# First attention: where the fp16 halves of the probabilities are made, and in what form they are turned

## The reference, cut to what matters

```
scores = einsum('bhsr,bhlr->bhsl', q_r, k_r)
attn = softmax(scores, axis=-1)
ctx_c = einsum('bhsl,bld->bhsd', attn, kv_rope)
ctx_lat = einsum('bhsd,hkd->bshk', ctx_c, w_kc_kv)
out = ctx_lat.reshape(b, s, H * K) @ Wo.T
```

## Time and profile before

| | |
|---|---|
| time, median of 3 runs | 1847.28 us (1844.83 to 1847.87) |
| the profiled execution: its time and its span | 1844.54 us, 1842.9 us |
| first attention in the span | about 130 to 680 us |
| busy in the whole span: TensorE, VectorE, ScalarE, GpSimd | 1606.8, 1192.0, 1036.1, 611.1 us |
| mean granted TensorE clock | 0.931 |
| L1051, all normalisations | 64, 137.3 us |

### The profile page before, as it was taken

One profiled execution on the slowest core, in us unless ns is written; L12 is line 12 of the kernel. 1 busy time (PEld: TensorE's weight loads), 2 busy tenths in 40 slices (PEclk: granted clock), 3 DMA queues, 4 the chain that ended last, 5 costly groups with the idle time before them and its releaser, 6 DMA issues. The chain is left out here.

```text
span 1842.9 us, 35610 instructions
## 1 busy us (share of the span) xinstructions
PE 1606.8 (87%) x11911; PEld 998.5 (54%) x11911; DVE 1192.0 (65%) x2678; ACT 1036.1 (56%) x2563; POOL 611.1 (33%) x481
## 2 busy tenths in 40 slices
PE   4788999999999979989997777784599999999993
PEld 3655656656656545555554454553466666666661
DVE  4866797787787779688796777757633333333332
ACT  3447746746747627566574777743655555455451
POOL 4614304304304300000000222212167777777662
PEclk9789999999999989999998998776599999999996
DMA  8820120220120249787786001104356656556536
GB/s 271 285 84 9 55 75 9 62 68 10 65 65 10 69 157 333 239 280 241 227 260 227 12 2 37 36 29 114 78 108 140 150 136 140 137 129 136 131 74 225
DMA packets 143332, 226.57 MB, mean 123 GB/s; under 512 B 37857, under 2 KB 93409, under 8 KB 143032
## 3 DMA queue, kind: packets, MB, share of 16 engines
q1 hardware_dynamic: 107160, 195.90, 33.6%
q0 software_dynamic: 29344, 21.29, 7.1%
q10 hardware_dynamic: 6656, 7.11, 1.1%
HBM read 175.00 MB, written 98.80 MB: 149 GB/s over the span
## 5 line engine op out<-in xcount | busy, mean ns | idle before, releaser
L2751 PE MATMUL g_ps<-ring,xT 128*128 x1572 | 300.8, 327 | 1.1 <-issue 1.1
L1051 POOL TENSOR_TENSOR pr<-pr,sm 128x1444 f32<-128x1444 f32 (+1 forms) x64 | 137.3, 2145 | 385.9 <-DVE sm L1087 385.9
L2700 POOL DMA_INDIRECT acc<-rows,slot_sources x131 | 207.8, 1586 | 107.2 <-issue 78.7
L2857 DVE SCALAR_TENSOR_TENSOR hf<-sg,g_ps 128x192 f32<-128x192 f32 x131 | 46.4, 354 | 238.5 <-ACT sg L2806 206.3
L2751 PEld LDWEIGHTS g_ps<-ring,xT 128*128 128x128 f16 x1572 | 142.8, 98 | 71.9 <-issue 5.5
L2690 POOL DMA_INDIRECT xg<-xtab,slot_sources x131 | 138.0, 1054 | 81.3 <-issue 79.5
L2773 PE MATMUL d_ps<-ring,hT 128*128 x655 | 162.8, 379 | 1.6 <-ACT hT L2819 1.1
L1081 DVE TENSOR_REDUCE sm<-s_banks 128x2 f32<-128x722 f32 (+2 forms) x128 | 97.5, 762 | 67.3 <-PE s_banks L819 64.8
L973 ACT ACTIVATE pr<-s_banks,sm 128x361 f32<-128x361 f32 (+1 forms) x208 | 115.3, 563 | 30.7 <-DVE sm L1081 29.2
L876 PE MATMUL o_bank<-cT,N_hi 128*128 128x400 f16 x512 | 129.7, 335 | 0.0
L819 PE MATMUL s_banks<-kvp,qp 128*128 128x361 f16 (+1 forms) x624 | 116.9, 318 | 10.8 <-ACT pr L973 6.1
(11 more groups left out here) (322 smaller groups left out, 3848.1 us busy)
## 6 DMA issues: line engine op xcount, KB each, us to landing
split_f<-in_gu SPq DMA_DIRECT2D x64, 384.0 KB, 4.5
split_gu<-split_o SPq DMA_DIRECT2D x64, 384.0 KB, 3.1
ring<-split_gu SPq DMA_DIRECT2D x32, 768.0 KB
head<-in_head SPq DMA_DIRECT2D x16, 864.0 KB
tern_w<-in_tern SPq DMA_DIRECT2D x48, 256.0 KB
split_f<-in_down SPq DMA_DIRECT2D x32, 384.0 KB, 4.2
split_d<-split_o SPq DMA_DIRECT2D x32, 384.0 KB, 3.8
ring<-split_d SPq DMA_DIRECT2D x32, 256.0 KB
```

What stands on the lines that cost most here:

```text
L1051: nc.gpsimd.tensor_tensor(pr[:, s % 3, 0:n], pr[:, s % 3, 0:n], small[:, s % 3, 2, 0:n].unsqueeze(2).to_broadcast([P, n, KEYS]), ALU.mult) ...
L2700: nc.gpsimd.indirect_dma_start(out=core.acc[i % NACC][:, :], out_offset=bass.IndirectOffsetOnAxis(ap=core.sources[:, i:i + 1], axis=0), in ...
L2751: last = nc.tensor.matmul(g_ps[i % 2][:, 0:2 * INTER], xT[:, i % 2, a * KT + k, :], ring(i, (2 * k + w) * 2 * INTER, 2 * INTER), start=((k ...
```

## The change

The split is made ahead of the transposition, on rows rather than on turned columns. After normalising, which is now two instructions a step (the first two tiles, then the rest), ScalarE copies each part to fp16 and GpSimd subtracts this copy from the fp32 probabilities into a second fp16 tile (new probs_hi and probs_lo, one instruction a part each). TensorE turns both fp16 halves of each tile, into the two halves of one bank that is read as fp16, so there are twice as many transpositions. VectorE then takes a bank's both halves in one copy (probs_out). The three slots of pr become two (probs0, probs1), with two for the fp16 parts (probs_parts). They lie over single ternary tiles in an order of their own, and some waits for the ternary tiles are set accordingly. An fp16 identity is written over the bf16 one for the duration of the stage and put back after it.

```diff
+ROW_PAD = 368
+TERN_ORDER = (("w", 0), ("w", 1), ("a", 0), ("s", 0), ("m", 0), ("a", 2), ("g", 2), ("s", 2), ("w", 2), ("g", 0), ("a", 1),
+              ("g", 1), ("m", 1), ("s", 1), ("m", 2), ("o", 1), ("o", 2), ("o", 0))
...
-        pad = tern.bytes // (3 * 4 * 4)
-        assert pad >= KEYS and STEPS % 3 == 1
-        pr = core.sb(ctx, "pr", [P, 3, 4, pad], F32)[:, :, :, 0:KEYS]
+        assert STEPS % 2 == 0
+        pr = [core.sb(ctx, f"probs{p}", [P, widest, KEYS], F32) for p, widest in enumerate((4, 3))]
+        ph = [core.sb(ctx, f"probs_parts{p}", [P, 2, widest, ROW_PAD], F16) for p, widest in enumerate((4, 3))]
+        core.sb(ctx, "tern_end", [P, tern.bytes // 4 - sum(w * (KEYS + ROW_PAD) + 8 for w in (4, 3))], F32)
...
-        pb = (tb[0], tb[1], ob[0])
+        pb = [bank[:, :].bitcast(F16).rearrange("p (a n) -> p a n", a=2) for bank in (tb[0], tb[1], ob[0])]
...
-                    sp.wait_ge(p_free.sem, p_free.after(c * STEPS + STEPS - 3))
+                    sp.wait_ge(parted.sem, parted.after(c * STEPS + STEPS - 2))
                     for u in range(2 * D):
+                        if u == D - 1:
+                            sp.wait_ge(p_turned.sem, p_turned.after(c * STEPS + STEPS - 2))
...
-                        pe.wait_ge(weighed.sem, weighed.after(c * STEPS + s))
+                        pe.wait_ge(parted.sem, parted.after(c * STEPS + s))
...
-                        last = nc.tensor.transpose(pb[u][0:KEYT[u], i * P:i * P + n],
-                                                   pr[0:n, s % 3, i, u * P:u * P + KEYT[u]],
-                                                   core.ident[0:n, 0:n])
+                        for a in range(2):
+                            last = nc.tensor.transpose(pb[u][0:KEYT[u], a, i * P:i * P + n],
+                                                       ph[s % 2][0:n, a, i, u * P:u * P + KEYT[u]], ident_h[0:n, 0:n])
...
+                    if e == 0 and c * STEPS + s >= 2:
+                        act.wait_ge(parted.sem, parted.after(c * STEPS + s - 2))
                     tiles = halves(s, e)
                     for i, n in tiles:
-                        nc.scalar.activation(pr[0:n, s % 3, i, :], sbank[0:n, i, 0:KEYS], ACT.Exp,
+                        nc.scalar.activation(pr[s % 2][0:n, i, :], sbank[0:n, i, 0:KEYS], ACT.Exp,
                                              bias=small[0:n, s % 3, 0, i:i + 1],
                                              accum_out=small[0:n, s % 3, 1, i:i + 1]
                                              ).then_inc(powered.sem, 2 // len(tiles))
 
-                def probs_hi(c, s, u):
-                    act.wait_ge(p_turned.sem, p_turned.after(c * STEPS + s, u + 1))
-                    n = width(s)
-                    nc.scalar.activation(pT[s % 2][0:KEYT[u], 0, u, 0:n], pb[u][0:KEYT[u], 0:n], ACT.Copy
-                                         ).then_inc(p_hi.sem, 1)
+                def probs_hi(c, s):
+                    if c * STEPS + s >= 2:
+                        act.wait_ge(p_turned.sem, p_turned.after(c * STEPS + s - 2))
+                    if c and s == 1:
+                        for k in range(1, D):
+                            act.wait_ge(tern.saved[k].sem, tern.saved[k].after(c * KT - 1))
+                    for e in range(2):
+                        n, at = half_of(s, e)
+                        act.wait_ge(normal.sem, normal.after(c * STEPS + s, e + 1))
+                        nc.scalar.activation(ph[s % 2][0:n, 0, at, 0:KEYS], pr[s % 2][0:n, at, :], ACT.Copy
+                                             ).then_inc(tile_hi.sem, 1)
...
-                        if 2 <= s < STEPS + 2:
-                            probs_hi(c, s - 2, 0)
-                            probs_hi(c, s - 2, 1)
                         if more and s == STEPS:
                             query_hi(c + 1, 0)
                         if more and s == STEPS + 1:
                             against_hi(c + 1, 0)
                         if s < STEPS:
                             exps(c, s, 0)
+                        if 1 <= s < STEPS + 1:
+                            probs_hi(c, s - 1)
...
-                    n = len(tiles_of(s % GROUPS))
-                    nc.gpsimd.tensor_tensor(pr[:, s % 3, 0:n], pr[:, s % 3, 0:n],
-                                            small[:, s % 3, 2, 0:n].unsqueeze(2).to_broadcast([P, n, KEYS]),
-                                            ALU.mult).then_inc(weighed.sem, 1)
+                    for e in range(2):
+                        n, at = half_of(s, e)
+                        probs, scale = pr[s % 2][0:n, at, :], small[0:n, s % 3, 2, at]
+                        nc.gpsimd.tensor_tensor(probs, probs, scale.unsqueeze(2).to_broadcast([n, at.stop - at.start, KEYS]),
+                                                ALU.mult).then_inc(normal.sem, 1)
+
+                def probs_lo(c, s):
+                    for e in range(2):
+                        n, at = half_of(s, e)
+                        pool.wait_ge(tile_hi.sem, tile_hi.after(c * STEPS + s, e + 1))
+                        last = nc.gpsimd.tensor_tensor(ph[s % 2][0:n, 1, at, 0:KEYS], pr[s % 2][0:n, at, :],
+                                                       ph[s % 2][0:n, 0, at, 0:KEYS], ALU.subtract)
+                    last.then_inc(parted.sem, 1)
 
                 for n in range(NCH * STEPS):
                     normalise(*divmod(n, STEPS))
+                    probs_lo(*divmod(n, STEPS))
...
-                def probs_lo(c, s, u):
-                    dve.wait_ge(p_hi.sem, p_hi.after(c * STEPS + s, u + 1))
+                def probs_out(c, s, u):
+                    dve.wait_ge(p_turned.sem, p_turned.after(c * STEPS + s, u + 1))
                     n = width(s)
-                    nc.vector.tensor_tensor(pT[s % 2][0:KEYT[u], 1, u, 0:n], pb[u][0:KEYT[u], 0:n],
-                                            pT[s % 2][0:KEYT[u], 0, u, 0:n], ALU.subtract).then_inc(p_free.sem, 1)
+                    nc.vector.tensor_copy(pT[s % 2][0:KEYT[u], :, u, 0:n], pb[u][0:KEYT[u], :, 0:n]).then_inc(p_free.sem, 1)
...
+                            dve.wait_ge(parted.sem, parted.after(c * STEPS + STEPS - 1))
...
-                        if 2 <= s < STEPS + 2:
-                            probs_lo(c, s - 2, 0)
                         if 1 <= s < STEPS + 1:
                             invert(c, s - 1)
                         if 2 <= s < STEPS + 2:
-                            probs_lo(c, s - 2, 1)
+                            probs_out(c, s - 2, 0)
+                            probs_out(c, s - 2, 1)
                         if more and s == STEPS:
```

More of the change, by code:

```diff
@@ L601, in __init__ @@
         self.o = [None] * D
-        self.s = core.sb(ctx, "tern_s", [P, D, DIM], BF16)
-        self.m = core.sb(ctx, "tern_m", [P, D, DIM], BF16)
-        self.o[0] = core.sb(ctx, "tern_o0", [P, DIM], BF16)
-        self.w = core.sb(ctx, "tern_w", [P, D, DIM], F32)
-        self.o[1] = core.sb(ctx, "tern_o1", [P, DIM], BF16)
-        self.a = core.sb(ctx, "tern_a", [P, D, DIM], BF16)
-        self.g = core.sb(ctx, "tern_g", [P, D, DIM], BF16)
-        self.o[2] = core.sb(ctx, "tern_o2", [P, DIM], BF16)
+        self.s, self.m, self.a, self.g, self.w = ([None] * D for _ in range(5))
+        for part, k in TERN_ORDER:
+            {"s": self.s, "m": self.m, "a": self.a, "g": self.g, "w": self.w, "o": self.o}[part][k] = core.sb(
+                ctx, f"tern_{part}{k}", [P, DIM], F32 if part == "w" else BF16)
         self.bytes = D * DIM * (5 * 2 + 4)
@@ L625, in round_off @@
         act.wait_ge(self.final.sem, self.final.room(n))
-        self.nc.scalar.activation(self.a[:, k, :], self.w[:, k, :], ACT.Abs).then_inc(self.rounded.sem, 1)
-        self.nc.scalar.activation(self.g[:, k, :], self.w[:, k, :], ACT.Sign).then_inc(self.rounded.sem, 1)
+        self.nc.scalar.activation(self.a[k][:, :], self.w[k][:, :], ACT.Abs).then_inc(self.rounded.sem, 1)
+        self.nc.scalar.activation(self.g[k][:, :], self.w[k][:, :], ACT.Sign).then_inc(self.rounded.sem, 1)
     def spread_sums(self, pe, j, k, bank):
@@ L631, in spread_sums @@
         pe.wait_ge(self.rounded.sem, self.rounded.after(n, 1))
-        self.nc.tensor.matmul(bank, self.core.gsum[:, :], self.a[:, k, :], start=True, stop=True
+        self.nc.tensor.matmul(bank, self.core.gsum[:, :], self.a[k][:, :], start=True, stop=True
                               ).then_inc(self.spread.sem, 1)
@@ L636, in ternary @@
         n = j * self.D + k
-        s, m, a, g = (v[:, k, :] for v in (self.s, self.m, self.a, self.g))
+        s, m, a, g = (v[k][:, :] for v in (self.s, self.m, self.a, self.g))
         dve.wait_ge(self.spread.sem, self.spread.after(n))
@@ L683, in attention0 @@
     powered = Steps(core, "exp_done", per=2)
-    inverse, weighed = Steps(core, "denominator_inverse"), Steps(core, "probs_normal")
-    p_turned, p_hi = Steps(core, "probs_turned", per=3), Steps(core, "probs_hi", per=3)
```

(18 more changed lines are left out.)

9 lines of the change are left out of this document (5 added, 4 removed).

## The result

The changed kernel takes 1922.05 us (median of 4 runs, 1915.88 to 1925.1) beside 1846.05 us for the kernel before (4 runs, 1842.36 to 1847.87): a ratio of 1.041, 95% interval 1.0379 to 1.0441. The profiled execution took 1925.1 us with a span of 1923.3, which is 80.4 more than the span of before. GpSimd's busy time rose from 611.1 to 778.2 us, the other engines' hardly moved, and the mean granted clock fell from 0.931 to 0.923.

A forecast was written before the change was run, and what follows sets the result against it. The prediction took a two-step loop through GpSimd, TensorE and VectorE to bound the changed kernel, 22.2 us for four steps. Its terms: 1844.5 + 72.7 (loop and pass ends) + 6 (clock) = 1923.2, left as 1923 us, range 1900 to 1945.

The forecast's parts named there:

- a loop two steps long through all the engines: First attention: GpSimd's last subtraction through TensorE and VectorE to normalising two steps on, 5.4 to 6.2 us, plus GpSimd's work.
- 72.7 + 6: First attention: 72.7 us more over four passes from the loop and pass ends, plus 6 us for clock drops.
- The instruction prices: Per-instruction costs on each engine, such as 1.56 us for GpSimd's subtraction of 722 elements, bounds 1.39 to 1.63.
- the reason that TensorE gains nothing: Turns on TensorE: two fp16 transpositions take 0.112 us against 0.117 for one fp32, saving 0.2 us in four steps.
- Four steps were put at 22.2 us: The loop in first attention: four steps were to take 22.2 us where they took 18.0.
- GpSimd's own 20.0: GpSimd's normalising and subtracting in four steps, 20.0 us; as the only bound, a rival at 1883 us.
- The total is about what it was: ScalarE: three copies from PSUM become two from SBUF, 0.80 us for 722 elements and 0.50 for 361.
- the rivals' sums for a cheaper subtraction: Subtraction on GpSimd: under about 1 us a step, two loop steps come under 9.15 us and TensorE's 16.4 us decides.
- faster: Rival: the split is hidden and TensorE runs without waiting, four steps 16.4 us, -28 us, 1817; chance 0.03.
- The ends of three passes: Ends of the first three passes: turn(15) comes 6.6 us after the last normalising begins, before 4.4: +2.3 each.
- +6 was a quarter of 16 waits: Clock on TensorE: +27 us if all 16 long waits brought a drop, 0 if none; a quarter taken, +6.
- happened at once: Reason for a quarter: TensorE's 2.21 us wait, once in a pass before the change, was followed by a clock drop.

The follow-up runs named there:

- 1: The changed kernel with the reciprocal of step s-1 ahead of the peaks of step s on VectorE: 1891.55 us, ratio to the kernel before 1.0252.
- 2: The changed kernel with GpSimd subtracting only 8 columns of each tile from step 2 of a pass on: 1904.76 us, ratio to the kernel before 1.0308.
- 6: The changed kernel with 8-column subtractions and ScalarE's context_hi(s-3) between its two copies instead of behind them: 1879.29 us, ratio to the kernel before 1.0177.
- experiment 7: The changed kernel, subtraction whole, with ScalarE's context_hi(s-3) between its two copies: 1924.83 us, ratio to the kernel before 1.0421.
- 9: The changed kernel with 8-column subtractions, reciprocal ahead of the next peaks and context_hi between ScalarE's copies: 1855.03 us, ratio to the kernel before 1.005.
- experiment 3: The changed kernel with 9, 3, 0 or 4 idle matmuls on TensorE ahead of a turn, into a free bank: 1916.1 us, ratio to the kernel before 1.0375.

## Why the prediction was right, and where it was not

The time came out within 1 us of the forecast, and the mechanism, a loop two steps long through all the engines, is the one that the runs show. That it came out so near is luck. Between the two traces first attention grew by 80.1 us where 72.7 + 6 = 78.7 was forecast; without the clock that is about 70 for 72.7, and the clock is 10 for 6, so that two errors partly cancel. And the forecast set out from the profiled execution of before, 1844.54, to name a median: the medians lie 76.0 us apart and the two profiled executions 80.4.

*Prices and loop.* The instruction prices held, and so did the reason that TensorE gains nothing: 12 fp16 transpositions take 0.84 us and 16 take 1.07, 0.057 each. Four steps were put at 22.2 us and took 21.89; GpSimd's own 20.0 are 19.1. The two-step loop is shown by both of its ends, since taking 0.9 us off VectorE's part (1) and taking the subtraction off GpSimd (2, then 6) each shortened the steps, and by experiment 7, where the other way was shortened and four steps stayed at 21.90. The Trainium skill's advice against this split (GPSIMD Engine Reference, "Engine selection") agrees in kind with the trace, though its ratio is about 2: 1.545 us for 722 elements is 1.6 times the 0.69 for 512 on VectorE, taken in proportion.

*The step that failed* inside it is the sentence "The total is about what it was" on ScalarE, with the exponentials put beside the rest: ScalarE was costed by its sum and not by its order. Its copies moved ahead of context_hi, and that made a second, one-step way round. In the changed kernel it and the two-step loop end within 0.1 us of each other behind the 4-tile step: the turn starts at 353.08 as the subtraction ends, and the reciprocal at 353.02, behind a context_lo that had waited 1.25 us for ScalarE. The trace of the changed kernel alone can't tell the two apart; experiments 2, 6 and 7 do. Each way by itself makes 11.03 us of the first two intervals (7 has only the loop, 2 only the one-step way). In the last two the loop decides, with 10.86 us for 10.4. Under the statistics the one-step way does, so that four of the 15 intervals of each later pass were set by a way that the prediction didn't have. It is also why the rivals' sums for a cheaper subtraction were wrong: "faster" was to be decided by a subtraction under 1 us a step, and at 0.4 us (2) the kernel is still 3.1% slower than before. Even with both orders mended (9) it doesn't come under before. Speed was further away than that rival supposed.

*The passes.* Without the six clock drops, that is with the filler of experiment 3, first to last normalising grew by 82.41 - 67.31 = 15.1 us in the first pass (14.9 predicted) and by 15.8, 15.8 and 15.4 in the later ones (16.1). The ends of three passes gave +2.2, +1.8 and +2.1 for 2.3. In the last pass the turn of step 15 came 4.77 us after the last normalisation began (4.7 predicted), as in the row below, whose partner is in the earlier trace rows, but the clock fell behind its wait, and the matmuls after it took 2.97 instead of 1.64 us. So that end cost 4.0 for 2.7.

```profile
702.69 1.05 PE L846 MATMUL t_bank<-ident_b,probs_parts 128*128 128x128 f16 x12 [2.02 <-POOL probs_parts L1080]
703.67 2.97 PE L859 MATMUL o_bank<-probsT,kvp 128*128 128x384 f16 x9
```

*The clock.* +6 was a quarter of 16 waits at 1.7 us (a quarter of 27 is 6.8; it was taken as 6). Measured: 8.8 for six drops in the loop and 1.3 for one at the end, about 10. Drops near a pass's beginning come on top (the kernel before has only one of them, about 150 us, and shorter), at some 0.3 us each in the second and third pass; in the first it wasn't separated. So the price of a drop was about right and their number too low. The reason given for a quarter, that such a wait "happened at once" to bring a drop, was too strong: the kernel before has this wait at three passes' ends, 2.21, 1.82 and 2.12 us, and the clock fell behind the first alone.

*The account.* First attention from its first piece to the next stage: 70.8 (first to last normalisings, clock included) + 6.1 + 4.0 - 0.8 (its start) = 80.1 of the 80.4 us between the two spans. Ahead of it the changed execution was 3.05 us quicker and behind it 3.4 us slower; both lie within the scatter of the runs and I haven't followed them up.

## What to carry to other kernels

Where two engines wait for each other in turn, list every way round with its length before pricing one; the second may lie a few tenths below the first, and then a cheaper operation gives back almost nothing. A moved instruction is costed by what it is now queued ahead of, not by its engine's sum. A small reordering inside a large change can be the part worth keeping: here one line of order gained 0.4% in the kernel before, while the change as a whole lost 4%.

## What I had not expected of the hardware

A wait of TensorE of a given length doesn't decide by itself whether the clock falls. In the first pass the granted clock stood at 1.00 before a wait of 1.96 us at 194.87 and fell to 0.50 behind it; in the second pass the wait ahead of the same step's turn was longer and the clock stayed at 1.00, so that four steps differ by some 1.6 us in passes that run the same instructions:

```profile
353.08 1.07 PE L846 MATMUL t_bank<-ident_b,probs_parts 128*128 128x128 f16 x16 [2.10 <-POOL probs_parts L1080]
...
354.00:354.50 0.50, 0.50 (x7) 0.38 (x5) 0.50 (x2) 0.33 (x2) 0.50 (x1) 1.00 0.06 16
```

And a subtraction on GpSimd has a floor, about the 0.18 us an instruction of the prediction: 16 elements a partition took 0.214 us where 722 took 1.545, so the least subtraction still cost a seventh of the full one.
